# A fused Mamba and mixture-of-experts block on one core: the prologue's small loads put on other queues, the condition transposed on TensorE

## What is computed

```python
mod = (_silu(L0_c) @ L0_wmod).reshape(8, 6, 1, -1)        
sa, ca, ga, sb, cb, gb = (mod[:, i] for i in range(6))
h = _layernorm(x) * (1 + ca) + sa
x = x + ga * attn(h)
h = _layernorm(x) * (1 + cb) + sb
x = x + gb * ffn(h)
```

## Time and profile before

| | |
|---|---|
| median of 3 runs | 2256.1 us (2250.99 to 2261.37) |
| the profiled execution, its own time | 2257.78 us |
| its span in the profile | 2255.8 us |
| PE busy | 2163.8 us (96%) |
| DVE busy | 1834.9 us (81%) |
| ACT busy | 1795.6 us (80%) |
| POOL busy | 1595.6 us (71%) |
| mean granted PE clock | 0.985 |

### The profile page before, as it was taken

One profiled execution on the slowest core, in us unless ns is written; L12 is line 12 of the kernel. 1 busy time (PEld: TensorE's weight loads), 2 busy tenths in 40 slices (PEclk: granted clock), 3 DMA queues, 4 the chain that ended last, 5 costly groups with the idle time before them and its releaser, 6 DMA issues. The chain is left out here.

```text
span 2255.8 us, 48650 instructions
## 1 busy us (share of the span) xinstructions
PE 2163.8 (96%) x14808; PEld 1848.3 (82%) x14808; DVE 1834.9 (81%) x4196; ACT 1795.6 (80%) x4208; POOL 1595.6 (71%) x1810
## 2 busy tenths in 40 slices
PE   4679999999999999999999999999999999999997
PEld 3568888888888888888888888888888888888875
DVE  4678888888888888888888888888888888888873
ACT  2578878888888888888888888888888888888862
POOL 1446767777777777777777777777777777777675
PEclk9699999999999999999999999999999999999999
DMA  4221221222222122122122222222222222222210
GB/s 120 65 75 53 70 81 60 81 77 70 62 81 80 61 81 81 60 72 81 60 81 76 69 63 81 78 63 83 79 60 72 81 64 77 76 64 68 72 57 19
DMA packets 154257, 160.86 MB, mean 71 GB/s; under 512 B 17200, under 2 KB 136592, under 8 KB 154000
## 3 DMA queue, kind: packets, MB, share of 16 engines
q1 hardware_dynamic: 148848, 157.71, 22.6%
q10 hardware_dynamic: 5152, 0.04, 0.1%
HBM read 139.88 MB, written 17.83 MB: 70 GB/s over the span
## 5 line engine op out<-in xcount | busy, mean ns | idle before, releaser
L897 DVE SCALAR_TENSOR_TENSOR feat<-pa,cw,feat 128x512 f32<-128x512 f32 x567 | 423.4, 747 | 54.1 <-ACT feat L603 45.8
L1300 PE MATMUL pe<-e_hi,h_hi 128*128 128x512 f32 x1024 | 435.5, 425 | 5.6 <-ACT ex L746 2.6
L1300 PE MATMUL pe<-e_lo,h_hi 128*128 128x512 f32 x1024 | 405.6, 396 | 0.0
L1300 PE MATMUL pe<-e_hi,h_lo 128*128 128x512 f32 x1024 | 405.5, 396 | 0.0
L1300 PE MATMUL pa<-h_hi,w_hi 128*128 128x260 f32 x1260 | 377.2, 299 | 8.2 <-DVE feat L897 7.0
L1300 PE MATMUL pa<-h_hi,w_lo 128*128 128x260 f32 x1260 | 358.3, 284 | 0.0
L1300 PE MATMUL pa<-h_lo,w_hi 128*128 128x260 f32 x1260 | 357.9, 284 | 0.0
L675 ACT ACTIVATE lm<-lm,lndt 128x128 f32<-128x128 f32 x1024 | 326.4, 393 | 1.9
L665 ACT ACTIVATE lm<-lm,e3in 128x128 f32<-128x128 f32 x1024 | 325.2, 394 | 0.9 <-DMA lm<-cs_rows 0.9
L603 ACT ACTIVATE feat<-pa,cb,cw 128x512 f32<-128x512 f32 x189 | 146.9, 777 | 188.6 <-PE pa L1300 188.0
L439 POOL TENSOR_TENSOR rs<-ssq,neghalf 128x1 f32<-128x1 f32 x128 | 85.6, 669 | 274.7 <-DVE ssq L1004 274.7
(11 more groups left out here) (181 smaller groups left out, 5912.8 us busy)
## 6 DMA issues: line engine op xcount, KB each, us to landing
lm<-cs_rows SPq DMA_DIRECT2D x128, 512.0 KB, 3.9
ebc<-cs_rows SPq DMA_DIRECT2D x256, 128.0 KB, 3.5
xin<-_attn_hidden_states_dram SPq DMA_DIRECT2D x32, 512.0 KB, 3.7
xres<-_attn_hidden_states_dram SPq DMA_DIRECT2D x128, 128.0 KB, 3.1
out_dram<-x SPq DMA_DIRECT2D x128, 128.0 KB, 2.7
gz<-in_L_wmod_dram SPq DMA_DIRECT2D x2, 512.0 KB, 8.7
ex<-in_L_ffn_expert_w_dram SPq DMA_DIRECT2D x1, 1024.0 KB, 16.9
x<-in_L_ffn_expert_w_dram SPq DMA_DIRECT2D x1, 1024.0 KB, 18.6
```

The source lines that it names most:

```text
L897: dve.scalar_tensor_tensor(out=acc, in0=proj_bank(x, i)[:, :, 1 + j:1 + j + HT], scalar=cw[:, f, j:j + 1], in1=acc, op0=ALU.mult, op1=ALU. ...
L1300: return pe.matmul(o, lhsT=l, rhs=r, start=start, stop=stop, skip_group_check=True)
```

## The change

The condition is loaded by ACT in one load of 8 rows of 1 KB into a scratch region (`c_rows`, a part of `eacc`), on a semaphore of its own, `s_cond`. ACT loads its silu table while it waits. PE transposes the rows into PSUM (`px`) with two matrix instructions, and ACT takes the silu from there. The silu no longer waits for `gz`; PE does.

The eight small loads are divided. `cw` and `cb` stay on ACT, but are issued behind the silu. `dtb_rep` and `a_rep` are issued by SP behind the first part of `feat`. These four are `s_vec`, and ACT waits for them behind `n_h` of both tile pairs, DVE where it did. `gb_rep`, `nw` and `d_fm` are issued by SP behind the expert weights, on `s_late`. ACT waits for that ahead of `wo_hi`, DVE ahead of `wo_lo`, and POOL ahead of the loop.

The twelve copies of `expert_b` leave SP and are issued by ACT, in six pairs, one pair behind each of `ca0` to `ca5`. The loop is the same.

```diff
-        cond = [(cT[:, k], c_in[:, k * P:(k + 1) * P].rearrange("b p -> p b")) for k in range(KT)]
-        vectors = [(cw[:], conv_w.rearrange("(f p) k -> p f k", p=P)), (cb[:], conv_b.rearrange("(f p) -> p f", p=P))]
-        for dst, src in ((dtb_rep, dt_bias), (a_rep, a_log), (gb_rep, gate_b)):
-            vectors.append((dst[:], src.rearrange("(o n) -> o n", o=1).to_broadcast([P, src.shape[0]])))
+        c_rows = eacc[0:NB, 3]
+        taps = [(cw[:], conv_w.rearrange("(f p) k -> p f k", p=P)), (cb[:], conv_b.rearrange("(f p) -> p f", p=P))]
+        heads = [(dst[:], src.rearrange("(o n) -> o n", o=1).to_broadcast([P, NH])) for dst, src in ((dtb_rep, dt_bias), (a_rep, a_log))]
+        n_vec = len(taps) + len(heads)
+        late = [(gb_rep[:], gate_b.rearrange("(o n) -> o n", o=1).to_broadcast([P, NE])), (nw[:], norm_w.rearrange("(f p) -> p f", p=P))]
...
-            sp.wait_ge(POOL0.sem, POOL0.at["bz"])
-            for r in bias_rows:
-                sp.dma_start(stage_b[r:r + NE], exp_b).then_inc(s_bias, 16)
-
+                if s_part is s_feat:
+                    for dst, src in heads:
+                        sp.dma_start(dst, src).then_inc(s_vec, 16)
+            for dst, src in late:
+                with nc.allow_non_contiguous_dma(reason="small vectors, once"):
+                    sp.dma_start(dst, src).then_inc(s_late, 16)
...
-            for dst, src in cond:
-                with nc.allow_non_contiguous_dma(reason="small vectors, once"):
-                    act.dma_start(dst, src).then_inc(s_c, 16)
-            for dst, src in vectors:
+            act.dma_start(c_rows, c_in).then_inc(s_cond, 16)
+            nc.scalar.preload_act_table_set("silu_and_others")
+            act.wait_ge(PE0.sem, PE0.at["cT"])
+            act.activation(scT[:].rearrange("p k b -> p (k b)"), px[:, 0, 0:KT * NB], ACT.Silu).then_inc(ACT0.sem, 1)
+            for dst, src in taps:
                 with nc.allow_non_contiguous_dma(reason="small vectors, once"):
                     act.dma_start(dst, src).then_inc(s_vec, 16)
-            loaded(act, s_c)
-            act.activation(scT[:], cT[:], ACT.Silu).then_inc(ACT0.sem, 1)
             act.wait_ge(DVE0.sem, DVE0.at["m11"])
-            act.wait_ge(s_vec, 16 * len(vectors))
...
+            def bias_loads(act, i):
+                for r in bias_rows[2 * i:2 * i + 2]:
+                    act.dma_start(stage_b[r:r + NE], exp_b).then_inc(s_bias, 16)
...
+            pe.wait_ge(s_cond, 16)
+            pe.wait_ge(POOL0.sem, POOL0.at["ident"])
+            for k in range(KT):
+                last = pe.transpose(px[:, 0, k * NB:(k + 1) * NB], c_rows[:, k * P:(k + 1) * P], ident[0:NB, 0:NB])
+            last.then_inc(PE0.sem, 1)
```

More of the change, by code:

```diff
@@ L169, in adaln_mamba_moe @@
         s_wo = sem("s_wo")
+        s_cond = sem("s_cond")
         s_vec = sem("s_vec")
+        s_late = sem("s_late")
         s_exp = sem("s_exp")
@@ L269, in adaln_mamba_moe @@
                                  exp_w[:, k * P:(k + 1) * P, :].rearrange("e p n -> p e n")))
-        cond = [(cT[:, k], c_in[:, k * P:(k + 1) * P].rearrange("b p -> p b")) for k in range(KT)]
-        vectors = [(cw[:], conv_w.rearrange("(f p) k -> p f k", p=P)), (cb[:], conv_b.rearrange("(f p) -> p f", p=P))]
-        for dst, src in ((dtb_rep, dt_bias), (a_rep, a_log), (gb_rep, gate_b)):
-            vectors.append((dst[:], src.rearrange("(o n) -> o n", o=1).to_broadcast([P, src.shape[0]])))
+        c_rows = eacc[0:NB, 3]
[3 more added lines that the diff above has]
+        late = [(gb_rep[:], gate_b.rearrange("(o n) -> o n", o=1).to_broadcast([P, NE])), (nw[:], norm_w.rearrange("(f p) -> p f", p=P))]
         d_halves = d_skip.rearrange("(o f two) -> o f two", o=1, two=2)
         for half in range(2):
-            vectors.append((d_fm[half * HD:(half + 1) * HD], d_halves[:, :, half].to_broadcast([HD, XT])))
-        vectors.append((nw[:], norm_w.rearrange("(f p) -> p f", p=P)))
+            late.append((d_fm[half * HD:(half + 1) * HD], d_halves[:, :, half].to_broadcast([HD, XT])))
         bias_rows = [(t * 32 + part * NE) for t in range(T) for part in range(3)]
         def loaded(eng, s_part):
-            eng.wait_ge(s_part, 16 * (len(loads[s_part]) + (len(cond) if s_part is s_c else 0)))
+            eng.wait_ge(s_part, 16 * len(loads[s_part]))
         @block.sync
@@ L498, in _ @@
                                        ALU.subtract).then_inc(POOL0.sem, 1)
-            pool.wait_ge(s_vec, 16 * len(vectors))
+            pool.wait_ge(s_late, 16 * len(late))
             pool.wait_ge(ACT0.sem, ACT0.at["g0"])
@@ L766, in _ @@
             do(ca0, act, 0)
+            act.wait_ge(POOL0.sem, POOL0.at["bz"])
+            bias_loads(act, 0)
             do(ca1, act, 0)
+            bias_loads(act, 1)
             do(ln_dt, act, 0)
             do(ca2, act, 0)
+            bias_loads(act, 2)
             do(csT_rows, act, 0)
@@ L772, in _ @@
             do(ca3, act, 0)
+            bias_loads(act, 3)
             do(si0, act, 0)
             do(ca4, act, 0)
+            bias_loads(act, 4)
             do(si1, act, 0)
             do(ca5, act, 0)
+            bias_loads(act, 5)
             e_first(act, 0)
@@ L784, in _ @@
             loaded(act, s_wo)
+            act.wait_ge(s_late, 16 * len(late))
             for k in range(XT):
@@ L1131, in _ @@
             do(n_hi, dve, 2)
-            dve.wait_ge(s_vec, 16 * len(vectors))
+            dve.wait_ge(s_vec, 16 * n_vec)
             do(dtb, dve, 0)
@@ L1183, in _ @@
                 dve.tensor_scalar(eb3[:, t], b_mix, tmask[:, t:t + 1], None, ALU.mult).then_inc(DVE0.sem, 1)
+            dve.wait_ge(s_late, 16 * len(late))
             for k in range(XT):
```

4 lines of the change are left out of this document (2 added, 2 removed).

## The result

The changed kernel takes 2240.2 us (median of 7 runs, 2236.03 to 2245.35) against 2256.1 (7 runs, 2250.37 to 2262.76) for the kernel before. The ratio is 0.9939, with an interval of 0.9922 to 0.9955, so the gain is 13.8 us by the ratio, and between 10.2 and 17.6. The medians differ by 15.9, the forecast was 12.4 (2243.7). The profiled execution after took 2236.03 (span 2234.3, mean granted clock 0.988); before it was 2257.78 (2255.8, 0.985).

What follows compares the result with a forecast made beforehand. TensorE was taken to bound the loop, so only the prologue could move, held by ACT's wait for small loads. 13.3 us gained less 0.85 for issues gave 12.4: 2256.1 - 12.4 = 2243.7 us, range 2236 to 2252.5.

Steps and rivals of the forecast that it cites:

- When `n_h` starts: Prologue, first `hf` on ACT: starts at 11.76 us instead of 25.06, a gain of 13.3 us.
- up to 1.3 more: Bound on the `n_h` gain: `gz` may land in 3.9 us, not 5.2, without the 4-byte pieces beside it.
- my bound of 8.2: Prologue, condition path: its new load lands by 7.2 and is through transposes and silu by 8.2; gain perhaps 1.2 less.
- The moved waits: ACT and DVE in the prologue: later waits for `s_vec` and `s_late` cost nothing; 1.3 us of cover at the dt bias.
- The rival that the small loads are as late as ever (2246.1): Last of `s_vec` lands at 25.06, dt bias waits 2.4 us more, gain is 10.0; chance 0.12.
- The issues on ACT: Six pairs of `expert_b` issues among ACT's feature blocks, 0.71 us a pair, lose 0.85 us in all.
- The lower bound that I gave: Price of the issue pairs on ACT is nothing, if its sequencer issues while the engine works on the activation ahead.
- not 1.6 as I had written: Sign of the issues' cost: DVE's taps of block 4 would wait some 1.6 us for ACT.
- The sum: Whole kernel: 13.3 gained less 0.85 lost is 12.4 us, so 2243.7 against 2256.1.
- The clock in the first passes: Rival on TensorE: shifted program meets clock changes elsewhere, -5.6 (2238.1) or +8.7 us (2252.4); chances 0.11 better, 0.10 worse.
- my two cases: TensorE's first passes: 12.12 us busy at the upper clock saves 5.6; 10.26 at the lower costs 8.7.
- the line at 0.5%: Whole kernel: below 2244.8 us, 11.3 less than before, it counts as faster; chance of faster 0.50.

Runs made afterwards that it cites:

- e11: The changed kernel a third time, with no edit, for another trace of the same program; 2241.1 us, ratio 0.9932.
- e3: The changed kernel with all eight small loads again issued by ACT behind the silu and waited for ahead of the first `hf`; 2258.17 us, ratio 1.0008.
- e8: The changed kernel with all twelve copies of `expert_b` issued by ACT in one row behind `ca3`; 2245.41 us, ratio 0.9950.
- e7: The changed kernel with ACT held before the first `hf` by 23 repeated activations, each waiting for the one before; 2259.21 us, ratio 1.0007.

## Why the prediction came out

**When `n_h` starts: right in its mechanism, 1.1 us too late.** I took 5.2 for `gz` and named "up to 1.3 more", if the 4-byte pieces had slowed it. They had: 4.1 to 4.8 without them, 5.2 to 5.3 with them. The modulation started at 6.02 and not at 7.1; the rest of the sum held (3.43 to the transposes, 1.09, 0.11 of hand-over). The condition was not late: its rows landed by 2.5, and with the silu at 2.91 PE could have started at about 3.2 (2.91 + 0.18 + 0.14), not at my bound of 8.2.

**The moved waits: free, as said, but not with the load that I named.** The dt bias at 21.61 waits for PE. I took `cb` for the last of the four, at 21.4, and gave no time to the two that went to SP; the last was `a_rep`, at 14.5 to 15.5 in the changed kernel's three traces, in e11 0.89 behind ACT's second `hf` pair. What kept that free is the 5.3 us or more that ACT idles behind the table load's exponential, and I had counted the cover on DVE alone. The rival that the small loads are as late as ever (2246.1) did not come about: `cw` took 5.5 and `dtb_rep` on SP 5.6 from its issue. The rule of the Trainium skill in "DMA: Bandwidth & Descriptors" (section "Issuing engines are not separate DMA queues"), from which I took that the move brings `dtb_rep` no earlier, spoke for that rival. The traces decide against what I made of it: `dtb_rep` issued at 4.07 on ACT landed 11.4 us later (e3), and issued at 3.29 on SP 5.6 later (after), so it was there 6.6 us earlier. But the rule grants the time to issue, and here that is most of it: the issue ended at 4.07 + 4.07 = 8.14 on ACT and at 3.29 + 0.47 = 3.76 on SP, 4.4 of the 6.6. So the traces don't contradict the rule; what they show is that the time to issue was not small. The sum with the late loads, 2246.1, lies 5.9 above the result. What made the other 2.2 us was not separated.

**The issues on ACT: 0.85 us forecast, nothing measured.** I added the length of each pair to ACT's work. The lower bound that I gave, nothing, "if ACT's sequencer issues while the engine still works on the activation ahead", was the right one, and e8 prices it: only what outlasts the activation counts. The taps of block 4 waited 0.90 us for ACT, as before (0.91), not 1.6 as I had written. DVE's timeline after:

```profile
39.92 2.33 DVE L911 SCALAR_TENSOR_TENSOR feat<-pa,cw,feat 128x512 f32<-128x512 f32 x3 [0.90 <-ACT feat L604]
```

**The sum.** 12.4 + 1.1 + 0.85 = 14.4, which is the shift of the first state product (14.44). The measured gains of 13.8, 15.8 and 15.3 agree with it; with intervals from 10.2 to 21.7 they would agree with the forecast's 12.4 as well, so it is the traces that tell the two apart. That the shift is the gain is shown by e7; that behind `hf` no load holds the chain in absolute time, by the 55.15 to 55.20 us in six traces with `hf` between 10.65 and 25.06.

**The clock in the first passes.** I priced it as a rival, -5.6 or +8.7, set by where the shifted program meets the changes. e7 was to show this: with the start of before it should have had the clock pattern of before. It did not (30.7 us at 1.2 GHz in the first 120 us, against 47.8). The traces alone leave it open, since the two of before (47.8, 47.7) lie above the three of after (34.1 to 40.9). All executions together settle it: over 22 of the changed kernel the mean granted clock was 0.986 (0.980 to 0.992), over the 63 of before that were measured beside the experiments 0.987 (0.980 to 0.992). The change brings no better clock. Within either kernel the time goes with that clock, some 1.8 us for each 0.001, and executions of the changed kernel alone reach from 2232.3 to 2252.9. So the clock is a spread of each execution, wider than my two cases together, and no effect of the change; that the gain came out near the forecast is not its doing. It moves single traces by several us: those of before and after differ by 21.5 us in span, 14.4 of them by the shift and the other 7 behind the first state product. Reading the gain off the two profiled executions would have overrated it by half.

**The chances.** A forecast 1.1 us from the line at 0.5% was a coin toss by construction, and part of its coming out is luck: the two mis-sized terms both erred on the cautious side (1.1 + 0.85 us), and the interval of the ratio still reaches over the line.

## What to carry to other kernels

Don't let an early step wait on one semaphore for a list of small loads whose last member is needed much later. Put each load on the semaphore of its first reader, and its issue where the issuing engine is idle: the wait moved alone gave 6.1 us, the silu brought forward alone nothing, both together 14. And to judge a prologue change of half a per cent, read the start of one instruction behind the prologue in several traces: with the granted clock at 1.00 for the first 39 us behind `hf`, the distance from `hf` repeated to 0.05 us, where the interval of the times is 7 us wide.

## What the hardware showed beyond that

- A DMA issue written behind an activation on ACT starts together with it. 0.31 to 0.34 us an issue, and only the part that outlasts the activation holds the engine (3.36 of 4.10 in e8).
- The same kind of small load takes 0.47 us to issue at one place and 4.07 at another. Both are `dtb_rep`, on SP in after and on ACT in e3. The long ones stand behind loads that are still on their way: `gb_rep` (3.03 on SP in after) behind the experts, `dtb_rep` on ACT behind `cw` and `cb`, whose pieces are small. The cause was not tested.
- With two 4 KB loads in pieces of 4 bytes beside them, the 256 KB loads `gz` landed in 5.2 to 5.3 us (four traces), without them in 4.1 to 4.8 (nine).
- One program met the 1.2 GHz level for 34.1, 37.5 and 40.9 us in its first passes in three executions, and thirteen traces spent 0.38 us more for each us at that level behind the first state product.
- `cw`, 12 KB, landed in 10.2 to 12.1 us where ACT issued all the other small loads behind it (four traces), and in 5.5 to 6.2 where ACT issued only `cb` behind it and SP the rest (eight). SP issues its weights up to 1 us later in these, so the two were not separated.
